# Splitting probabilities earlier in the first attention steps of a fused transformer block on Trainium2

## What is computed

```
x = x + L0_xattn(layernorm(x), ctx)
x = x + L0_ffn(layernorm(x))
q = rope(layernorm(x) @ wq)            # 32 heads of 128
k = rope(ctx @ wk); v = ctx @ wv       # 8 heads of 128
attn = softmax(q k^T / sqrt(128) + mask)
x = x + (attn v) @ wo
x = x + L1_ffn(layernorm(x))
```

## Time and profile before

| | us |
|---|---|
| median of 3 runs | 1749.76 (1749.03 to 1750.7) |
| the profiled execution's own time | 1747.76 |
| its span in the trace | 1745.9 |
| PE busy, DVE busy | 1707.5, 1114.5 |
| ACT busy, POOL busy | 768.0, 896.2 |
| granted TensorE clock, mean | 0.997 |

### The profile page before, as it was taken

One profiled execution on the slowest core, in us unless ns is written; L12 is line 12 of the kernel. 1 busy time (PEld: TensorE's weight loads), 2 busy tenths in 40 slices (PEclk: granted clock), 3 DMA queues, 4 the chain that ended last, 5 costly groups with the idle time before them and its releaser, 6 DMA issues.

```text
span 1745.9 us, 26098 instructions
## 1 busy us (share of the span) xinstructions
PE 1707.5 (98%) x8784; PEld 1558.1 (89%) x8784; DVE 1114.5 (64%) x2192; ACT 768.0 (44%) x1609; POOL 896.2 (51%) x695
## 2 busy tenths in 40 slices
PE   7999999999999999999899999999999999999998
PEld 6999999999888888888799989889999999999986
DVE  7631275556533233334778888898888888888845
ACT  5211211012423332323222233488888888888724
POOL 3324522114522212111687874488887887878734
PEclk9999999999999999999999999999999999999999
DMA  5222333234734333433334445577777777777643
GB/s 134 61 60 84 127 118 107 81 98 134 229 112 129 121 110 118 130 111 96 104 104 113 122 128 147 138 208 197 192 192 191 192 192 192 192 192 193 163 110 108
DMA packets 177198, 241.37 MB, mean 138 GB/s; under 512 B 47312, under 2 KB 145872, under 8 KB 176064
## 3 DMA queue, kind: packets, MB, share of 16 engines
q1 hardware_dynamic: 177088, 239.99, 49.4%
HBM read 142.68 MB, written 46.92 MB: 109 GB/s over the span
## 4 chain that ended last, share of the span: by engine, by line
PE 80%; DVE 3%; POOL 2%; issue 1%; DMA 1%; ACT 1%; SPq 0%; DVEq 0%; ACTq 0%; POOLq 0%
PE bank L200 76%; POOL x_sums_low L1602 1%; PE bank L106 1%; PE bank L2583 1%; PE bank L186 1%; PE bank L2596 1%; POOL shared_operand_low L328 1%; DMA aw_weights_then_ctx_rows<-in_wk 0%; POOL w_rest_low L793 0%; PE bank L1286 0%; DVE q_crossed L858 0%; DVE q_crossed L857 0%; DVE e_scores L1963 0%; PE bank L1283 0%; PE bank L2566 0%
## 5 line engine op out<-in xcount | busy, mean ns | idle before, releaser
L328 POOL TENSOR_TENSOR shared_operand_low<-ctx_raw,shared_operand_high 128x768 fp32r<-128x768 f32 x64 | 119.4, 1877 | 198.2 <-ACT shared_operand_high L324 198.1
L200 PE MATMUL bank<-shared_operand_high,w_first_high 128*128 128x448 f32 (+1 forms) x568 | 205.9, 362 | 11.6 <-POOL w_first_low L1609 8.6
L200 PE MATMUL bank<-shared_operand_low,w_first_high 128*128 128x448 f32 (+1 forms) x568 | 204.9, 361 | 0.0
L200 PE MATMUL bank<-shared_operand_high,w_first_low 128*128 128x448 f32 (+1 forms) x568 | 204.7, 360 | 0.0
L1971 ACT ACTIVATE e_scores<-e_scores,e_least 128x375 f32<-128x375 f32 x256 | 153.0, 599 | 38.2 <-DVE e_least L1963 38.0
L324 ACT ACTIVATE shared_operand_high<-ctx_raw 128x768 fp32r<-128x768 f32 x64 | 52.8, 842 | 210.6 <-DMA ctx_raw<-in_ctx_t 192.1
L1963 DVE CUSTOM_DVE_ANT_0 e_scores<-bank,e_mask_then_layer_ffn 128x375 f32<-128x375 f32 x256 | 134.9, 530 | 0.0
L200 PE MATMUL bank<-shared_operand_high,w_rest_high 128*128 128x376 f32 x384 | 128.8, 335 | 1.5 <-POOL w_rest_low L793 1.5
L200 PE MATMUL bank<-shared_operand_high,w_rest_low 128*128 128x376 f32 x384 | 128.6, 335 | 0.0
L200 PE MATMUL bank<-shared_operand_low,w_rest_high 128*128 128x376 f32 x384 | 128.6, 335 | 0.0
L200 PEld LDWEIGHTS bank<-shared_operand_high,w_first_high 128*128 128x128 f32 x568 | 107.5, 189 | 19.5 <-issue 9.0
(11 more groups left out here) (324 smaller groups left out, 5076.9 us busy)
## 6 DMA issues: line engine op xcount, KB each, us to landing
ctx_raw<-in_ctx_t SPq DMA_DIRECT2D x64, 384.0 KB, 3.8
e_shuffled_then_xn_t<-q_rotated_then_x_rows SPq DMA_DIRECT2D x128, 192.0 KB, 3.6
e_shuffled<-q_rotated_then_x_rows SPq DMA_DIRECT2D x128, 192.0 KB, 3.6
e_raw_wo<-in_wo SPq DMA_DIRECT2D x64, 256.0 KB, 4.0
aw_weights_then_ctx_rows<-in_wq SPq DMA_DIRECT2D x30, 512.0 KB, 4.2
q_rotated<-q_rotated_then_x_rows SPq DMA_DIRECT2D x64, 224.0 KB, 2.4
e_raw_then_a<-q_rotated SPq DMA_DIRECT2D x64, 224.0 KB, 3.8
v_rows<-v_out SPq DMA_DIRECT2D x48, 256.0 KB, 2.5
```

The lines of the kernel that those rows point to most:

```text
L200: mm = pe.matmul(out, stationary[a], moving[b], start=(first and i == 0), stop=(last and i == 2))
L328: pool.tensor_tensor(k.ctx_ring[1][slot][:, 2 * j:2 * j + 2, :], k.c_raw[:, j % 2], f32(k.ctx_ring[0][slot][:, 2 * j:2 * j + 2, :]), ALU.s ...
```

## The change

Three lists are written in another order; no instruction is added, removed or resized.

- ScalarE, steps 1 to 4: `normalise_last` follows the rounding of the probabilities instead of preceding it (step 0 had that order already).
- VectorE, steps 1 to 4: `probabilities_low(s)` comes right behind `take_output(s - 1)`, ahead of the first L1963, instead of behind the first transpose. In step 4 it follows the scaling of head 0.
- VectorE, steps 3 and 4: the last rotation, `rotate(3)`, leaves the end of step 3; step 4 runs its inverse sums, then `take_output(3)`, then `rotate(3)`, then the scaling of head 0.

```diff
-            if 0 < s < STEPS - 2:
+            if FILLED < s < STEPS - 2:
                 first.normalise_last(act, s + 2, u)
             act.wait_ge(first.shuffled[s % 2], 64 * (s // 2) + 64)
             for c in range(KEY_TILES):
                 act.activation(by_block(pt[0][:, c, :]), raw_p(s, c), ACT.Copy).then_inc(pt_high, 1)
-            if s == 0:
-                first.normalise_last(act, 2, u)
+            if s <= FILLED:
+                first.normalise_last(act, s + 2, u)
...
             if probabilities:
                 first.invert(dve, s + 2, u)
+            if s == FILLED:
+                take_output(s - 1)
+                last_heads.rotate(dve, s - 1)
+            if probabilities:
                 first.normalise(dve, s + 2, u, (0,))
-            if s >= 1:
+            if s >= 1 and s != FILLED:
                 take_output(s - 1)
+            if 0 < s <= FILLED:
+                probabilities_low(s)
             if scores:
                 first.mask_scores(dve, s + AHEAD, (u + AHEAD) % BATCH, (0,))
...
-            if s:
+            if s > FILLED:
                 probabilities_low(s)
...
-            if s < FILLED:
+            if s < FILLED - 1:
                 last_heads.rotate(dve, s)
-            else:
+            elif s >= FILLED:
                 add_y(s, u, 0)
                 add_y(s, u, 1)
```

## The result

The changed kernel takes 1751.78 us in the median of 20 runs (1750.22 to 1753.81), the kernel before 1749.32 us in 20 runs beside it (1746.79 to 1751.82). The ratio is 1.0015 with a 95% interval of 1.0008 to 1.0021: 2.5 us slower, which is within the 0.2% that the prediction counts as no change, but its interval lies wholly above 1. The profiled execution took 1750.27 us, its span is 1748.4 us (before: 1747.76 and 1745.9).

A forecast was written before the change was run, and what follows sets the result against it. VectorE leads in attention steps 0 to 4, TensorE afterwards. New collisions and VectorE's lateness, partly absorbed by slack, sum to +0.3 to +2.5 us, taken as +1.3: 1749.76 + 1.3 = 1751.1 us, range 1746.3 to 1754.5.

The forecast's parts named there:

- The heart: Steps 1 and 2: VectorE's step, 8.4 us before, grows to about 9.6 and becomes longer than TensorE's 8.9.
- my sum: Total effect on the kernel after steps 5 to 7: +0.3 to +2.5 us, taken as +1.3.
- part 1: Steps 1 to 3, earlier L2248 and rounding: GpSimd collisions add 1.1 us to VectorE in each of steps 1 and 2.
- TensorE's waits, steps 1 to 3: Total wait for L2248 falls to about 0.8 us; wait for L1963 rises from 0.5 to 2.
- Part 2: Step 4, attended values ahead of the last rotation: L2243 and project +0.3 us, VectorE's last L1963 +3.3 us.
- Part 3: Steps 5 to 7: the 3.3 us debt uses up L2248's 2.6 us slack; TensorE starts +0.3 to +1.3 us in step 5.
- a sign in step 5: Sign of being right: a TensorE wait for L2248 appears in step 5.
- a sign of being wrong: The forecast counts as wrong if nothing waits in step 5.
- The pace holds: Rival: no new collisions, VectorE's step stays 8.4 us, all but the first wait go, 1743.7 us; chance 0.08.
- half the debt: Rival: one collision per step, VectorE 1 us late after step 3, clock stays up, -2.0 us, 1747.8; chance 0.17.
- The debt persists: Rival: VectorE needs 9.7 us a step in steps 5 to 7, second 1.2 GHz stretch, +4.6 us, 1754.4; chance 0.13.
- The bound of 6.1 us: Most the change could win before 1161 us: TensorE's waits for low parts and 1.7 us lost at half clock, 0.35%.

The follow-up runs named there:

- e4: Changed kernel with GpSimd's two probability parts in steps 1 to 3 held until VectorE's L2248 of the step is done: 1751.0 us against 1748.93, ratio 1.0010.
- e12: The kernel before run again with no edit, for a second trace: 1749.35 us, ratio 1.0002.
- e3: The kernel before with only the last rotation moved into step 4 behind take_output: 1749.93 us against 1748.93, ratio 1.0006.
- e11: The changed kernel run again with no edit, for a second trace: 1751.75 us against 1749.03, ratio 1.0014.
- e1: Changed kernel with step 4's output-weight parts on ScalarE and GpSimd made right after the probability parts: 1753.36 us against 1748.93, ratio 1.0028.
- e6: e5 with VectorE's L2248 of step 4 right behind the scaling of head 0: 1751.24 us, ratio 1.0012 against the kernel before.
- e10: Kernel before with GpSimd's probability parts behind L2248 (steps 5-7), weight parts before value part (steps 4-6), last rotation moved into step 4: 1748.2 us, ratio 0.9998.
- e7: The kernel before with GpSimd's probability parts of steps 5 to 7 waiting for VectorE's L2248: 1748.5 us against 1748.83, ratio 0.9998.
- e5: e3 with GpSimd's probability parts of steps 5 to 7 waiting for VectorE's L2248: 1749.33 us against 1748.83 for the kernel before, ratio 1.0004.

## Why the prediction was right, and where it wasn't

The forecast was 1751.1 us, slower by 1.3 but within 0.2%, with VectorE's step growing past TensorE's. It came to 1751.78. The heart holds; the place where the loss comes out was another, and its size twice mine: +2.46, at the very top of the +0.3 to +2.5 of my sum. That the time itself is only 0.7 us off is partly luck: I started from 1749.76, the median of three runs, and over 20 runs the kernel before takes 1749.32.

- **The collision (part 1).** Predicted 0.8 us for the scaling of head 0 and 0.3 for L2248; measured 0.68 (1.10 less 0.42) and 0.30 (1.04 less 0.74). e4 shows by taking GpSimd away that both are collisions. The Trainium skill, page "SBUF — State Buffer", section "Who interferes with whom", says that between GpSimd and VectorE in a two-port mode whichever issues first holds the shared ports for its whole instruction. The trace agrees for the scaling: it asked 0.26 us after GpSimd's first part began and ended 0.2 us after that part's end (1125.12 against 1124.95, half of the pair).
- **VectorE's step.** Predicted 9.6 us (its own terms, 8.4 + 1.1, give 9.5); it is 9.39 in steps 1 and 2, above TensorE's 8.9. Step 1's last L1963 was forecast for 1130.7 and ended there within 0.3. For step 3 I had +2.2; it became +1.4, as step 3 itself got 0.5 shorter (9.96 us against 10.46), where I had put nothing. VectorE's rows say why, in step 3 before (first two) and changed:

```profile
1139.96 1.34 DVE L1666 TENSOR_TENSOR q_rotated_then_x_rows<-q_straight,q_crossed 128x448 f32<-128x448 f32 x1
...
1143.59 1.31 DVE L1984 TENSOR_SCALAR e_scores<-e_scores,e_inv 128x375 f32<-128x375 f32 x1
...
1141.79 0.89 DVE L1666 TENSOR_TENSOR q_rotated_then_x_rows<-q_straight,q_crossed 128x448 f32<-128x448 f32 x1
...
1145.93 0.82 DVE L1984 TENSOR_SCALAR e_scores<-e_scores,e_inv 128x375 f32<-128x375 f32 x1
```


  The sum in SBUF that ends the rotation (L1666) and the scaling of head 1 (L1984) are 0.45 and 0.49 us shorter, L2248 is 0.46 longer (1.04 against 0.58). I had looked at the scalings only and taken them as hit alike. Part of it is scatter: the kernel before takes 10.23 us for step 3 in e12, and e3, with the same order up to there, 9.44.
- **TensorE's waits, steps 1 to 3.** L2248 fell from 2.2 to 0, not to 0.8. L1963 rose to 1.5, not 2.
- **Part 2.** L2243 of step 4 came 0.4 us earlier instead of 0.3 later, since step 3 ended at +1.4 instead of +2.2. The idle time of 2.0 us stayed as forecast. I kept the half clock behind it: it was absent in the first trace and there in e11, so it can go either way, and as e11 and e12 show, the sum stays the same.
- **Part 3, where the mechanism failed.** I had a debt of 3.3 us at the end of step 4 (it is 2.4) and let the slack of 2.6 us at L2248 of step 5 swallow most of it, leaving +0.3 to +1.3. Two things were wrong. The slack that counts is that of the weights' low parts, which hang on the same L1963 by way of ScalarE and GpSimd: 1.4 us, not 2.6 (e1, e6, and the rule for W5). And steps 5 to 7 don't pay a debt back: with double weight parts VectorE needs 9.5 us a step there (e11, e12, e3, e4), so nearly the whole 2.4 reaches the end. The wait for L2248 that I had named as a sign in step 5 came in neither trace of the changed kernel: in the first the wait there is for the weights, and in e11 nothing waits, which I had named as a sign of being wrong.
- **The rivals.** "The pace holds" and "half the debt" are out; e4, with about one collision a step, is the second of them and is still 1.4 us slower than before in its trace. "The debt persists" was right on VectorE's pace (9.7 predicted, 9.5 seen) and wrong that this comes on top: the kernel before runs at this pace too when TensorE gets ahead (e12). Its second stretch at half clock came in the changed kernel's first trace, but in place of the one in step 4.
- **The bound of 6.1 us.** I counted waits and half clock as winnable, since "time that TensorE wins before 1161 is won to the end". e12's trace refutes that sentence: it has the half clock gone, 1.6 us won at V5 and none of it at V12, so those 1.7 us were not to be won.

What stays open: what decides whether the clock falls, why step 3's length scatters by 1 us between traces of one order, and whether a debt of 2.4 us, and not only e10's 1.2, could be carried.

## What to carry to other kernels

When an engine follows another closely, a wait removed from the follower can merely move, as it did here; read the slack to the next thing that hangs on the leader, along every engine in between, and not only on the instruction that comes next on the leader itself. A wait on several semaphores must be checked against the code: here the named releaser was no operand of the waiting matmul. And before counting lost time as gain, look for a later stretch in which the leading engine has no room, since what is won ahead of it can be paid back there, as in e12.

## What was not expected of the hardware

- The clock is not a function of the idle time just ahead alone. Behind an idle time of 2.16 us (before) the granted clock is 0.51 for 3.4 us; behind 2.19 us at the same place (e7, e12) it stays at 1.00. Behind 1.97 us it stays up in the changed kernel and in e1, and behind 1.96 us it falls in e11. Behind 1.81 us it falls in e3, behind 1.74 at the same place it stays up in e5. The stretch lasts 3.4 us in the trace of before, but 6 us in e11 and 6.8 (at 0.55 in the mean) in e6.
- What one engine costs the other depends on who asks first. An early GpSimd start by 2.4 us made one VectorE instruction 0.68 us and another 0.30 us longer, and held back (e4) it moved the 0.65 us to the next scaling; GpSimd's own busy time hardly changed (894.9 us, before 896.2).
